# Sorted expert tiles: hidden units on the partitions, expert weights as the stationary operand

## The chip, the cores and the metric

The kernel runs on one core of a Trainium2 chip. The metric is the device time of one execution in microseconds; a time is the median of several runs. Engines run in parallel and meet at semaphores: TensorE (PE in the profile, its weight loads PEld), VectorE (DVE), ScalarE (ACT), GpSimd (POOL) and SyncE (SP), which issues DMAs. TensorE's granted clock stands in the profile as a share of 2.4 GHz: 1.00 is 2.4 GHz and 0.50 is 1.2 GHz, its two levels.

## The reference

Two graph layers, each followed by an expert network, run over 6250 rows of 256 numbers. The change lies in the last network, in which every row goes to the one expert of 32 that its router chooses:

```python
xf = x.reshape(-1, D)                              # layer-normed rows, D = 256
idx = jnp.argmax(xf @ router_w.T + router_b, axis=-1)
h = jnp.einsum('nd,ndh->nh', xf, W1[idx]) + b1[idx]   # 64 hidden units
h = jax.nn.relu(h)
out = jnp.einsum('nh,nhd->nd', h, W2[idx]) + b2[idx]
out = jax.nn.relu(out)                             # and x + out is the result
```

## The kernel before, in words

The kernel is written by hand, engine by engine: each block gives every engine its own list of instructions, and only semaphores order them between engines. Its stages follow one another: node features and edge scores, attention over the edges, the first expert network, the second sum over the edges (a gather stage, to about 2600 us in the profile), then `mean_route` and `expert_tiles`.

`mean_route` finishes the second graph layer, normalises it and routes the rows. In its first block SyncE loads the router's weights RWN, the vectors GA and BE and the router's bias RBB on one queue (L2136 to L2139). TensorE waits for both router loads before it transposes the router's weights (L2242). A middle part transposes and multiplies the rows for the router (L2356, L2368, L2380). At the end VectorE works out the place of every row in a list that is sorted by expert, padded to 128 rows for each expert, and for each of the TL = 80 tiles of that list the expert's number times 64 (TE1) and times 256 (TE2). GpSimd scatters the rows to that list in HBM (`rows_by_expert`, 49 indirect DMAs, L2303). The first-layer weights of all experts stand in SBUF as M1 (256 input features in two halves on the partitions, 32 x 64 columns), the second-layer weights and bias as M2 (64 + 1 partitions, 32 x 256 columns).

`expert_tiles` is the sorted-tile loop. SyncE first loads the first-layer bias of all experts, copied to all 128 partitions (B1B, L2538), and then keeps 16 tiles of 128 rows in flight (L2544). For each tile VectorE normalises (L2640), TensorE transposes both halves (L2566), ScalarE copies them to SBUF (xT, L2618), and TensorE multiplies with the tokens as stationary operand and the expert's 64 columns of M1 as moving operand, at an address from a register (L2578). So the product has tokens on its partitions. VectorE adds the bias (L2650), TensorE transposes the hidden rows (L2586), ScalarE applies the relu (L2626), and TensorE multiplies by the second layer (L2596), where a row of ones in hT brings in the bias b2. Ahead of that it computes another product of 256 columns into the other half of the same bank, which nothing reads (L2595). VectorE applies the relu and adds the row (L2657), and GpSimd scatters the result to its place in the output (L2551). Turn j of TensorE's loop works on four tiles: it transposes tile j, runs the first layer of tile j - 1, the hidden transpose of tile j - 2 and the second layer of tile j - 3. Every 16 tiles TensorE and VectorE load 16 registers each with the tiles' addresses (`load`). Buffers: two of xT, h, hT and of each PSUM tile, four of the outputs O and their row numbers ID.

All matrix products are in fp32; one such product stands in the trace as two records, a transpose as one.

Of the kernel before, what the change touches and what calls it, by code (L numbers as in the profile page):

```python
# [111 lines left out]
def program(nc, x, src, dst, edge_attr, W_fc, W_e, attn_h, attn_e, attn_t, bias, sW1, sb1, sW2, sb2, sW3, sb3,  # L112
# [16 lines left out]
    with ctx:  # L129
# [79 lines left out]
        POSI = sb(ctx, "POSI", [128, RB], i32)  # L209
        TE1 = sb(ctx, "TE1", [1, TL], i32)  # L210
# [3 lines left out]
        with phase():  # L214
            put = mean_route(nc, sb, ps, sem, sems, ACC, WM, IDF, RDQ, REAL, SKIPF, gamma, beta, W1, W2, b2, M1, M2, GX, ST, MEAN, RSTD,
                             ident, iota, below, epsc, router_w, router_b, POSI, TE1, TE2, SORTD)
            expert_tiles(nc, sb, ps, sem, sems, SORTD, put, TE1, TE2, M1, b1, M2, ident, out)

# [1872 lines left out]
def mean_route(nc, sb, ps, sem, sems, ACC, WM, IDF, RDQ, REAL, SKIPF, gamma, beta, W1, W2, b2, M1, M2, GX, ST, MEAN, RSTD, ident, iota,  # L2091
               below, epsc, router_w, router_b, POSI, TE1, TE2, SORTD):
# [11 lines left out]
    with ExitStack() as s:  # L2104
# [22 lines left out]
        with ExitStack() as one:  # L2127
# [5 lines left out]
            with nc.Block() as block:  # L2133
                @block.sync
                def _(sp):
                    sp.dma_start(RWN[:, :], router_w[:, :]).then_inc(rw_in, 16)  # L2136
                    sp.dma_start(GA[:, :], gamma.rearrange("(k p) -> p k", p=128), allow_slow_non_contiguous=True).then_inc(w_in, 16)
                    sp.dma_start(BE[:, :], beta.rearrange("(k p) -> p k", p=128), allow_slow_non_contiguous=True).then_inc(w_in, 16)
                    sp.dma_start(RBB[:, :], router_b.partition_broadcast(128)).then_inc(rw_in, 16)  # L2139
                    sp.wait_ge(w_in, 32)  # L2140
                    sp.wait_ge(rw_in, 32)

                @block.vector
                def _(dve):
# [38 lines left out]
                    dve.wait_ge(w_in, 32)  # L2183
# [93 lines left out]
        with nc.Block() as block:  # L2277
# [120 lines left out]
            def _(dve):  # L2398
# [101 lines left out]
                nc.vector.tensor_scalar(TEG[:, :], TEF[:, :], float(NE - 1), float(EH), ALU.min, ALU.mult)  # L2500
                dve.drain()
# [7 lines left out]

def expert_tiles(nc, sb, ps, sem, sems, SORTD, put, TE1, TE2, M1, b1, M2, ident, out):  # L2510

    S = 4
    TS = 16
    RG = 16
    with ExitStack() as s:
        B1B = sb(s, "B1B", [128, NE * EH])
# [11 lines left out]
        b_in, one_set = sem("b1_in"), sem("hT_ones")  # L2528
# [3 lines left out]
        h_psum, h_ready, r_psum, r_ready = sem("sh_psum"), sem("sh_ready"), sem("shT_psum"), sem("shT_ready")  # L2532
        o_psum, o_ready = sem("so_psum"), sem("so_ready")

        with nc.Block() as block:
            @block.sync
            def _(sp):
                sp.dma_start(B1B[:, :], b1.rearrange("e h -> (e h)").partition_broadcast(128)).then_inc(b_in, 16)  # L2538

                sp.wait_ge(put, 16 * RB)  # L2540
                for j in range(TL):
                    if j >= TS:
                        sp.wait_ge(o_ready, j - TS + 1)
                    sp.dma_start(T[j % TS][:, :], SORTD[j * 128:(j + 1) * 128, :]).then_inc(t_in[j % TS], 16)  # L2544
                sp.wait_ge(b_in, 16)
# [11 lines left out]
            def _(pe):  # L2557
                regs1 = [pe.alloc_register(f"te1_{m}") for m in range(RG)]
# [23 lines left out]
                def turn_hidden(j):  # L2582
                    pe.wait_ge(h_ready, j + 1)
                    if j >= 2:
                        pe.wait_ge(r_ready, j - 1)
                    nc.tensor.transpose(pR[j % 2][0:EH, 0:128], h[j % 2][:, :], ident[:, :]).then_inc(r_psum, 1)  # L2586

                def second_layer(j):
# [3 lines left out]
                    pe.wait_ge(r_ready, j + 1)  # L2592
                    if j >= 2:
                        pe.wait_ge(o_ready, j - 1)
                    nc.tensor.matmul(pO[j % 2][:, D:2 * D], xT[j % 2][:, 0:128], M1[:, 0, 0:D], start=True, stop=True)  # L2595
                    nc.tensor.matmul(pO[j % 2][:, 0:D], hT[j % 2][:, :],  # L2596
                                     M2[:, :, :].rearrange("h e d -> h (e d)")[:, ds(r, D)],
                                     start=True, stop=True).then_inc(o_psum, 1)

                pe.wait_ge(one_set, 2)  # L2600
                for j in range(TL + 3):
# [4 lines left out]
                    if 0 <= j - 2 < TL:  # L2606
                        turn_hidden(j - 2)
                    if 0 <= j - 3 < TL:
                        second_layer(j - 3)

            @block.scalar
            def _(act):
                for j in range(TL + 2):
                    if j < TL:
                        act.wait_ge(t_ready, j + 1)
                        if j >= 2:
                            act.wait_ge(h_psum, j - 1)
                        nc.scalar.activation(xT[j % 2][:, :], pT[j % 2][:, 0:KD * 128], ACT.Copy).then_inc(x_ready, 1)  # L2618
                    n = j - 2
                    if 0 <= n < TL:  # L2620
                        act.wait_ge(r_psum, n + 1)
                        if n >= 2:
                            act.wait_ge(o_psum, n - 1)
                        else:
                            act.wait_ge(one_set, 2)
                        nc.scalar.activation(hT[n % 2][0:EH, :], pR[n % 2][0:EH, 0:128], ACT.Relu).then_inc(r_ready, 1)  # L2626

            @block.vector
            def _(dve):
                for k in range(2):  # L2630
                    nc.vector.memset(hT[k][EH:EH + 1, :], 1.0).then_inc(one_set, 1)
                regs = [dve.alloc_register(f"tb1_{m}") for m in range(RG)]
                dve.wait_ge(b_in, 16)
# [9 lines left out]
                def hidden(j):  # L2643
                    if j % RG == 0:
                        dve.load(regs, TE1[0:1, j:j + RG])
                    r = dve.snap(regs[j % RG], min_val=0, max_val=(NE - 1) * EH)
                    dve.wait_ge(h_psum, j + 1)
                    if j >= 2:
                        dve.wait_ge(r_psum, j - 1)
                    nc.vector.tensor_tensor(h[j % 2][:, :], pH[j % 2][:, 0:EH], B1B[:, ds(r, EH)], ALU.add).then_inc(h_ready, 1)  # L2650

                def finish(j):
# [4 lines left out]
                    nc.vector.scalar_tensor_tensor(O[j % S][:, :], pO[j % 2][:, 0:D], 0.0, T[j % TS][:, 0:D],  # L2657
# [35 lines left out]
```

## Time and profile before

| | |
|---|---|
| median of 3 runs | 3021.5 us (3019.42 to 3024.75) |
| the profiled execution | 3018.93 us, span 3017.1 us |
| busy over the span | PE 2261.7 us (75%), PEld 1908.8 (63%), POOL 1837.4 (61%), DVE 1745.5 (58%), ACT 1283.2 (43%) |
| sorted-tile loop | from about 2857 us to the end of the span |

The shares are means over stages that have different limits, so what bears on the change is the stretch of the sorted-tile loop. Times in views count from the start of the span. A group's row gives the busy time of all its instructions, the mean of one in ns, and the idle time of its engine just before them with what ended it. A matmul's record includes the time until its result is out, so consecutive ones overlap; the chain of waits counts only what each adds. The columns of a window are: its stretch, its length, the busy us of PE, PEld, DVE, ACT and POOL with the number of their records, the granted clock, the mean busy share of the 16 DMA engines, and GB/s.

### The profile page before, as it was taken

What the parts mean: (1) busy time and instruction counts of PE and PEld (TensorE: products, weight loads), DVE (VectorE), ACT (ScalarE), POOL (GpSimd) and SP (SyncE); (2) the same over time, 40 slices, a digit from 0 to 9 for tenths busy, and PEclk for the clock granted to TensorE, in tenths of its full rate; (3) what the DMA queues carried; (4) which work ended last, traced back from release to release, by engine and by line L of the source; (5) the groups of instructions that cost most, each with busy time, mean ns of one, the idle gap of its engine ahead of it and who ended that gap; (6) DMA issues with size and microseconds to landing.
All of it is one profiled execution on the core that took longest, in us unless ns stands there. A gap on an engine that the chain in (4) does not pass through costs nothing. (4 is left out here: it accounts for less than half of the span.)

```text
span 3017.1 us, 46958 instructions
## 1 busy us (share of the span) xinstructions
PE 2261.7 (75%) x12072; PEld 1908.8 (63%) x12072; DVE 1745.5 (58%) x5695; ACT 1283.2 (43%) x4568; POOL 1837.4 (61%) x1935
## 2 busy tenths in 40 slices
PE   5987667666766666699994887788878887874098
PEld 4886566666665555588873665666666666763087
DVE  6433888888888888677763333333333333567054
ACT  1533555555555454455563333333333333442033
POOL 5575777777777777421216777777777777300655
PEclk8999788888888788899995657655665666787599
DMA  7698444444444445520002333333333333103342
GB/s 211 176 224 232 111 112 112 112 111 112 113 112 112 112 111 131 169 65 15 29 15 91 105 106 106 105 106 106 105 106 106 105 106 106 49 1 57 127 122 80
DMA packets 250114, 323.65 MB, mean 107 GB/s; under 512 B 152723, under 2 KB 181001, under 8 KB 249335
## 3 DMA queue, kind: packets, MB, share of 16 engines
q0 software_dynamic: 89424, 235.59, 27.7%
q1 hardware_dynamic: 155784, 82.05, 11.4%
q10 hardware_dynamic: 4640, 3.02, 0.5%
q8 instruction: 100, 1.64, 0.2%
q14 instruction: 166, 1.36, 0.1%
HBM read 276.41 MB, written 48.24 MB: 108 GB/s over the span
## 5 line engine op out<-in xcount | busy, mean ns | idle before, releaser
L1526 PE MATMUL pAb<-HOTb,Gb 128*128 128x128 f32 x3136 | 811.5, 412 | 203.9 <-DMA Gb<-normed_rows,SRCT 154.0
L1505 POOL DMA_INDIRECT Gb<-normed_rows,SRCT x784 | 741.3, 946 | 248.9 <-issue 238.5
L1526 PEld LDWEIGHTS pAb<-HOTb,Gb 128*128 128x128 f32 x3136 | 633.5, 286 | 382.3 <-DMA Gb<-normed_rows,SRCT 297.5
L1566 DVE TENSOR_TENSOR ACC<-ACC,pAb 128x256 f32 x784 | 330.5, 422 | 642.2 <-PE pAb L1526 569.1
L1093 POOL DMA_INDIRECT GX<-ft_rows,SRCT x432 | 413.1, 956 | 131.5 <-issue 129.0
L1179 ACT ACTIVATE ACC<-apA 128x254 f32 x784 | 300.4, 383 | 409.4 <-PE apA L1252 335.0
L1252 PE MATMUL apA<-AHOT,GX 128*128 128x129 f32 x1920 | 302.0, 326 | 83.5 <-DVE GX L1401 83.1
L1545 ACT ACTIVATE HOTb<-OFFb 128x1024 f32<-128x1024 f32 x98 | 103.6, 1057 | 604.4 <-PE pAb L1526 604.2
L1252 PEld LDWEIGHTS apA<-AHOT,GX 128*128 128x128 f32 x1920 | 286.7, 238 | 102.6 <-DVE GX L1401 102.6
L1093 POOL DMA_INDIRECT G<-ft_rows,SRCT x288 | 274.5, 953 | 87.6 <-issue 84.8
L1541 ACT ACTIVATE OFFb<-iota,NRELb 128x128 f32<-128x128 f32 x784 | 239.6, 388 | 6.7
L1252 PE MATMUL apA<-AHOT,G 128*128 128x129 f32 x1216 | 196.0, 332 | 50.6 <-DVE G L1401 48.6
L1252 PEld LDWEIGHTS apA<-AHOT,G 128*128 128x128 f32 x1216 | 186.0, 243 | 62.6 <-DVE G L1401 60.1
L1694 POOL DMA_INDIRECT normed_rows<-nrow,IDI x49 | 50.1, 1022 | 252.6 <-ACT nrow L1923 239.1
L1401 DVE TENSOR_TENSOR GX<-GX,apV 128x1024 f32<-128x1024 f32 x120 | 143.1, 1192 | 0.0
L1180 ACT ACTIVATE FL<-apA 128x4 f32<-128x4 f32 x784 | 135.1, 172 | 0.0
L2303 POOL DMA_INDIRECT rows_by_expert<-GX,POSI x49 | 48.6, 993 | 135.4 <-DVE POSI L2490 120.7
L2551 POOL DMA_INDIRECT out_dram<-sO,sID x80 | 77.7, 972 | 77.7 <-issue 40.9
L1301 DVE TENSOR_TENSOR AHOT<-apL,RELT 128x1024 f32<-128x1024 f32 x98 | 118.6, 1210 | 0.0
L2618 ACT ACTIVATE sxT<-spT 128x256 f32<-128x256 f32 x80 | 30.7, 383 | 164.5 <-PE spT L2566 164.5
L520 PE MATMUL pS<-VB,eT 128*128 128x128 f32 x784 | 98.6, 280 | 0.5 <-ACT V L617 0.5
L1159 ACT ACTIVATE ACC<-VAL 128x2 f32 x792 | 89.8, 196 | 11.9 <-ACT FL L1180 10.8
(416 smaller groups left out, 3981.6 us busy)
## 6 DMA issues: line engine op xcount, KB each, us to landing
ebuf<-in_edge_attr_dram SPq DMA_DIRECT2D x49, 448.0 KB
Gb<-normed_rows,SRCT POOLq DMA_INDIRECT x784, 2.7
rows_by_expert<-ffn_PADT SPq DMA_DIRECT2D x1, 10360.0 KB, 45.0
sT<-rows_by_expert SPq DMA_DIRECT2D x80, 129.5 KB, 2.1
GX<-ft_rows,SRCT POOLq DMA_INDIRECT x480
ft_rows<-row SPq DMA_DIRECT2D x25, 231.0 KB
GX<-in_x_dram SPq DMA_DIRECT2D x10, 560.0 KB
G<-ft_rows,SRCT POOLq DMA_INDIRECT x304
```

The costliest lines, as they stand in the source:

```text
L520: last = nc.tensor.matmul(pS[:, m * 2 * H0:m * 2 * H0 + 128], eT[c % 2][:, m * EP:(m + 1) * EP], VB[:, :], start=True, stop=True)
L1093: pool.indirect_dma_start(G[c % GS][:, m, :], None, FT[:, :], bass.IndirectOffsetOnAxis(ap=SRCT[:, t:t + 1], axis=0)).then_inc(g_in[c % GS ...
L1179: nc.scalar.activation(acc[:, :, ds(r + 1, EP - 1)], sums[:, :, 1:EP], ACT.Copy)
L1180: nc.scalar.activation(FL[:, :, f:n + 1:n - f], sums[:, :, 0:HW:EP], ACT.Copy).then_inc(pfree[b], 1)
L1252: last = nc.tensor.matmul(pA[b][:, f * HW:(f + 1) * HW], G[c % GS][:, m, f * 128:(f + 1) * 128], HOT[c % 2][:, m, :], start=True, stop=True)
L1301: nc.vector.tensor_tensor(HOT[c % 2][:, h * HT:(h + 1) * HT, 0:EP], pL[0:EP, 256:256 + EP].unsqueeze(1).to_broadcast([EP, HT, EP]), RELT[: ...
L1401: nc.vector.tensor_tensor(v, v, pV[0:EP, 0:128].rearrange("p (h m) -> p h m", m=UT)[:, :, m:m + WB].rearrange("p h m -> p m h").unsqueeze( ...
L1505: pool.indirect_dma_start(G[g % R][m][:, :], None, TABLE[:, :], bass.IndirectOffsetOnAxis(ap=SRCT[:, t:t + 1], axis=0)).then_inc(g_in[g % ...
L1526: last = nc.tensor.matmul(pA[b][:, o:o + EP], G[k][m][:, c * 128:(c + 1) * 128], HOT[k % 2][:, m, :], start=True, stop=True)
L1541: nc.scalar.activation(OFF[k2][:, m, :], iota[0:EP, 0:EP], ACT.Abs, bias=NREL[k2][:, m:m + 1])
L1545: nc.scalar.activation(HOT[k2][:, :, :], OFF[k2][:, :, :], ACT.Relu, bias=1.0, scale=-1.0).then_inc(hot[k2], 1)
L1566: last = nc.vector.tensor_tensor(acc[:, :, ds(b, EP)], acc[:, :, ds(b, EP)], pA[q][:, o:o + KD * EP].rearrange("p (c r) -> p c r", c=KD), ...
```

## The change

The first layer's product is turned round: for each tile ScalarE copies the expert's first-layer weights (128 partitions x 2 x 64 numbers) from M1 to a buffer WU, and the two 128x64 halves of WU become the stationary operand, with the 128 transposed tokens as moving operand. The product has the hidden units on its partitions, so the transpose of the hidden rows goes (with it L2586, pR and h), and so does VectorE's bias addition: ScalarE's relu reads the product from PSUM and takes the expert's bias as a column of B1T, a transposed copy of b1 with 64 partitions and 32 columns, addressed by the expert's plain number (TE0). SyncE loads B1T in the first block of `mean_route`, behind RWN and ahead of GA, BE and RBB; the broadcast load of B1B goes. The product that nothing reads goes. The loop has three stages in place of four; xT, hT, WU, pH and pO have three buffers, O, ID and xn six. The register load for the first layer moves from TensorE to ScalarE, and the one for the bias from VectorE to ScalarE.

The diff, cut to its core (the remaining lines pass B1T and TE0 through and rename semaphores):

```diff
 # program
+        B1T = sb(ctx, "B1T", [EH, NE])
+        TE0 = sb(ctx, "TE0", [1, TL], i32)
 # mean_route, first block, SyncE
                     sp.dma_start(RWN[:, :], router_w[:, :]).then_inc(rw_in, 16)
+                    sp.dma_start(B1T[:, :], b1.rearrange("e h -> h e"), allow_slow_non_contiguous=True).then_inc(w_in, 16)
 ...
-                    sp.wait_ge(w_in, 32)
+                    sp.wait_ge(w_in, 48)
 # mean_route, first block, VectorE
-                    dve.wait_ge(w_in, 32)
+                    dve.wait_ge(w_in, 48)
 # mean_route, end, VectorE
                 nc.vector.tensor_scalar(TEG[:, :], TEF[:, :], float(NE - 1), float(EH), ALU.min, ALU.mult)
+                nc.vector.tensor_scalar(TE0[:, :], TEF[:, :], float(NE - 1), None, ALU.min)
 # expert_tiles
-    S = 4
+    S = 6
+    W = 3
-        B1B = sb(s, "B1B", [128, NE * EH])
-        xT = [sb(s, f"sxT{k}", [128, KD * 128]) for k in range(2)]
-        h = [sb(s, f"sh{k}", [128, EH]) for k in range(2)]
-        hT = [sb(s, f"shT{k}", [EH + 1, 128]) for k in range(2)]
+        xT = [sb(s, f"sxT{k}", [128, KD * 128]) for k in range(W)]
+        WU = [sb(s, f"sWU{k}", [128, KD, EH]) for k in range(W)]
+        hT = [sb(s, f"shT{k}", [EH + 1, 128]) for k in range(W)]
-        pH = [ps(s, f"spH{k}", [128, 512]) for k in range(2)]
-        pR = [ps(s, f"spR{k}", [128, 512]) for k in range(2)]
-        pO = [ps(s, f"spO{k}", [128, 512]) for k in range(2)]
+        pH = [ps(s, f"spH{k}", [128, 512]) for k in range(W)]
+        pO = [ps(s, f"spO{k}", [128, 512]) for k in range(W)]
 # SyncE
-                sp.dma_start(B1B[:, :], b1.rearrange("e h -> (e h)").partition_broadcast(128)).then_inc(b_in, 16)
 # TensorE
                 def first_layer(j):
-                    if j % RG == 0:
-                        pe.load(regs1, TE1[0:1, j:j + RG])
-                    r = pe.snap(regs1[j % RG], min_val=0, max_val=(NE - 1) * EH)
                     pe.wait_ge(x_ready, j + 1)
-                    if j >= 2:
-                        pe.wait_ge(h_ready, j - 1)
+                    if j >= W:
+                        pe.wait_ge(h_ready, j - W + 1)
                     for c in range(KD):
-                        last = nc.tensor.matmul(pH[j % 2][:, 0:EH], xT[j % 2][:, c * 128:(c + 1) * 128], M1[:, c, ds(r, EH)],
-                                                start=(c == 0), stop=(c == KD - 1))
+                        last = nc.tensor.matmul(pH[j % W][0:EH, 0:128], WU[j % W][:, c, :],
+                                                xT[j % W][:, c * 128:(c + 1) * 128], start=(c == 0), stop=(c == KD - 1))
                     last.then_inc(h_psum, 1)
-                def turn_hidden(j):
 ...
-                    nc.tensor.transpose(pR[j % 2][0:EH, 0:128], h[j % 2][:, :], ident[:, :]).then_inc(r_psum, 1)
                 def second_layer(j):
 ...
-                    nc.tensor.matmul(pO[j % 2][:, D:2 * D], xT[j % 2][:, 0:128], M1[:, 0, 0:D], start=True, stop=True)
+                    nc.tensor.matmul(pO[j % W][:, 0:D], hT[j % W][:, :], M2[:, :, :].rearrange("h e d -> h (e d)")[:, ds(r, D)],
                                      start=True, stop=True).then_inc(o_psum, 1)
-                for j in range(TL + 3):
+                for j in range(TL + 2):
                     if j < TL:
                         turn(j)
                     if 0 <= j - 1 < TL:
                         first_layer(j - 1)
                     if 0 <= j - 2 < TL:
-                        turn_hidden(j - 2)
-                    if 0 <= j - 3 < TL:
-                        second_layer(j - 3)
+                        second_layer(j - 2)
 # ScalarE
-                for j in range(TL + 2):
+                regs = [act.alloc_register(f"tb1_{m}") for m in range(RG)]
+                regs1 = [act.alloc_register(f"te1_{m}") for m in range(RG)]
+                for j in range(TL + 1):
                     if j < TL:
+                        if j >= W:
+                            act.wait_ge(h_psum, j - W + 1)
+                        if j % RG == 0:
+                            act.load(regs1, TE1[0:1, j:j + RG])
+                        r = act.snap(regs1[j % RG], min_val=0, max_val=(NE - 1) * EH)
+                        nc.scalar.activation(WU[j % W][:, :, :], M1[:, :, ds(r, EH)], ACT.Copy)
                         act.wait_ge(t_ready, j + 1)
-                        if j >= 2:
-                            act.wait_ge(h_psum, j - 1)
-                        nc.scalar.activation(xT[j % 2][:, :], pT[j % 2][:, 0:KD * 128], ACT.Copy).then_inc(x_ready, 1)
-                    n = j - 2
+                        nc.scalar.activation(xT[j % W][:, :], pT[j % 2][:, 0:KD * 128], ACT.Copy).then_inc(x_ready, 1)
+                    n = j - 1
                     if 0 <= n < TL:
-                        act.wait_ge(r_psum, n + 1)
+                        if n % RG == 0:
+                            act.load(regs, TE0[0:1, n:n + RG])
+                        e = act.snap(regs[n % RG], min_val=0, max_val=NE - 1)
+                        act.wait_ge(h_psum, n + 1)
 ...
-                        nc.scalar.activation(hT[n % 2][0:EH, :], pR[n % 2][0:EH, 0:128], ACT.Relu).then_inc(r_ready, 1)
+                        nc.scalar.activation(hT[n % W][0:EH, :], pH[n % W][0:EH, 0:128], ACT.Relu,
+                                             bias=B1T[:, ds(e, 1)]).then_inc(h_ready, 1)
 # VectorE
-                def hidden(j):
 ...
-                    nc.vector.tensor_tensor(h[j % 2][:, :], pH[j % 2][:, 0:EH], B1B[:, ds(r, EH)], ALU.add).then_inc(h_ready, 1)
                 norm(0)
-                for j in range(TL + 3):
+                for j in range(TL + 2):
                     if j + 1 < TL:
                         norm(j + 1)
-                    if 0 <= j - 1 < TL:
-                        hidden(j - 1)
-                    if 0 <= j - 3 < TL:
-                        finish(j - 3)
+                    if 0 <= j - 2 < TL:
+                        finish(j - 2)
```

## Rows read from the trace of the kernel before

**Rows 1.** Chain of waits, one tile: start us, length us, engine, line.
```profile
2901.20 0.22 PE spT L2566 x2
2901.42 0.39 PE spH L2578 x4
2901.81 0.11 PE spR L2586
2901.92 0.43 PE spO L2595 x2
2902.35 0.43 PE spO L2596 x2
```

**Rows 2.** Chain of waits, longest pieces of the span; columns alike.
```profile
2857.07 4.79 DMA sT<-rows_by_expert
...
2869.44 0.85 PE spO L2596 x2
...
2895.65 0.65 PE spH L2578 x4
...
2922.65 0.65 PE spH L2578 x4
```

**Rows 3.** Windows: stretch, length, busy us by engine, clock, DMA share, GB/s.
```profile
2877.00:2878.00 1.00, 1.00 (x7) 0.97 (x7) 0.48 (x3) 0.50 (x2) 0.26 (x1) 0.70 0.03 6
2895.00:2915.00 20.00, 18.85 (x129) 16.93 (x130) 11.58 (x48) 7.67 (x24) 10.89 (x12) 1.00 0.42 120
```

**Rows 4.** Groups, 2865 to 3005: busy us, mean ns, idle before, releaser.
```profile
L2657 DVE SCALAR_TENSOR_TENSOR sO<-spO,sT 128x256 f32<-128x256 f32 x80 | 33.9, 424 | 53.3 <-PE spO L2596 53.3
...
L2640 DVE TENSOR_SCALAR sxn<-sT 128x256 f32<-128x256 f32 x77 | 31.1, 404 | 0.0
...
L2655 DVE CAST sID<-sT 128x1 int32<-128x1 f32 x80 | 11.5, 143 | 0.1
...
L2618 ACT ACTIVATE sxT<-spT 128x256 f32<-128x256 f32 x78 | 29.9, 383 | 70.7 <-PE spT L2566 70.7
...
L2626 ACT ACTIVATE shT<-spR 64x128 f32<-64x128 f32 x80 | 21.6, 270 | 17.2 <-PE spR L2586 8.9
```

**Rows 5.** Timeline of the loop: start us, length us, instruction, idle before.
```profile
2871.58 0.97 POOL L2551 DMA_INDIRECT out_dram<-sO,sID  x1 [19.22 <-DVE sO L2657]
...
2995.29 0.42 DVE L2657 SCALAR_TENSOR_TENSOR sO<-spO,sT 128x256 f32<-128x256 f32 x1 [0.59 <-PE spO L2596]
...
2996.50 0.97 POOL L2551 DMA_INDIRECT out_dram<-sO,sID  x1 [0.62 <-issue]
...
3006.79 0.97 POOL L2551 DMA_INDIRECT out_dram<-sO,sID  x1 [0.31 <-issue]
```

**Rows 6.** Groups by shape, ScalarE, whole span; columns as rows 4.
```profile
L1939 ACT ACTIVATE e<-fpM,ffn_C 128x256 f32<-128x256 f32 x144 | 67.2, 474 | 55.3 <-PE fpM L2034 31.1 <-PE fpM L2041 24.1
...
L1133 ACT ACTIVATE U_ex<-U_own 128x128 f32<-128x128 f32 x49 | 15.3, 312 | 0.0
```

**Rows 7.** DMA issues of the page: count, KB each, us to landing.
```profile
sT<-rows_by_expert SPq DMA_DIRECT2D x80, 129.5 KB, 2.1
```

**Rows 8.** Window at the opening of the mean stage.
```profile
2603.00:2608.00 5.00, 4.56 (x11) 3.69 (x12) 1.80 (x6) 2.57 (x5) 0.00 (x0) 0.51 0.12 15
```

**Rows 9.** Timeline of the same opening.
```profile
2605.00 0.47 SPq L2139 DMA_DIRECT2D RBB<-in_L_ffn_router_b_dram  x1
...
2610.80 0.31 PE L2242 MATMUL rpL<-ident,RWN 32*128 32x32 f32 x2
```

**Rows 10.** Windows in the gather stage and the router stage.
```profile
2475.00:2480.00 5.00, 2.80 (x16) 2.04 (x16) 2.11 (x5) 0.61 (x1) 3.78 (x5) 1.00 0.37 105
2480.00:2485.00 5.00, 3.99 (x17) 3.06 (x17) 1.27 (x3) 2.99 (x10) 3.78 (x5) 0.66 0.36 105
...
2682.00:2692.00 10.00, 7.25 (x58) 6.28 (x57) 7.04 (x25) 6.13 (x13) 0.00 (x0) 1.00 0.00 0
2692.00:2697.00 5.00, 1.21 (x11) 0.96 (x10) 4.31 (x11) 0.36 (x1) 0.00 (x0) 0.97 0.02 3
```

More of the change, by code:

```diff
@@ L215, in program @@
             put = mean_route(nc, sb, ps, sem, sems, ACC, WM, IDF, RDQ, REAL, SKIPF, gamma, beta, W1, W2, b2, M1, M2, GX, ST, MEAN, RSTD,
-                             ident, iota, below, epsc, router_w, router_b, POSI, TE1, TE2, SORTD)
-            expert_tiles(nc, sb, ps, sem, sems, SORTD, put, TE1, TE2, M1, b1, M2, ident, out)
+                             ident, iota, below, epsc, router_w, router_b, POSI, b1, B1T, TE0, TE1, TE2, SORTD)
+            expert_tiles(nc, sb, ps, sem, sems, SORTD, put, TE0, TE1, TE2, M1, B1T, M2, ident, out)
 def constants(nc, sem, ident, iota, below, epsc, FIRSTI):
@@ L2091, in mean_route @@
 def mean_route(nc, sb, ps, sem, sems, ACC, WM, IDF, RDQ, REAL, SKIPF, gamma, beta, W1, W2, b2, M1, M2, GX, ST, MEAN, RSTD, ident, iota,
-               below, epsc, router_w, router_b, POSI, TE1, TE2, SORTD):
+               below, epsc, router_w, router_b, POSI, b1, B1T, TE0, TE1, TE2, SORTD):
     K = 5
@@ L2507, in mean_route, with expert_tiles @@
     return put
-def expert_tiles(nc, sb, ps, sem, sems, SORTD, put, TE1, TE2, M1, b1, M2, ident, out):
-    S = 4
+def expert_tiles(nc, sb, ps, sem, sems, SORTD, put, TE0, TE1, TE2, M1, B1T, M2, ident, out):
+    S = 6
+    W = 3
     TS = 16
@@ L2531, in expert_tiles @@
         xn_ready, t_ready, x_ready = sem("sxn_ready"), sem("sxT_psum"), sem("sxT_ready")
-        h_psum, h_ready, r_psum, r_ready = sem("sh_psum"), sem("sh_ready"), sem("shT_psum"), sem("shT_ready")
+        h_psum, h_ready = sem("shT_psum"), sem("shT_ready")
         o_psum, o_ready = sem("so_psum"), sem("so_ready")
@@ L2544, in _ @@
                     sp.dma_start(T[j % TS][:, :], SORTD[j * 128:(j + 1) * 128, :]).then_inc(t_in[j % TS], 16)
-                sp.wait_ge(b_in, 16)
             @block.gpsimd
@@ L2557, in _ @@
             def _(pe):
-                regs1 = [pe.alloc_register(f"te1_{m}") for m in range(RG)]
                 regs2 = [pe.alloc_register(f"te2_{m}") for m in range(RG)]
@@ L2591, in second_layer @@
                     r = pe.snap(regs2[j % RG], min_val=0, max_val=(NE - 1) * D)
-                    pe.wait_ge(r_ready, j + 1)
-                    if j >= 2:
-                        pe.wait_ge(o_ready, j - 1)
-                    nc.tensor.matmul(pO[j % 2][:, D:2 * D], xT[j % 2][:, 0:128], M1[:, 0, 0:D], start=True, stop=True)
-                    nc.tensor.matmul(pO[j % 2][:, 0:D], hT[j % 2][:, :],
-                                     M2[:, :, :].rearrange("h e d -> h (e d)")[:, ds(r, D)],
+                    pe.wait_ge(h_ready, j + 1)
+                    if j >= W:
+                        pe.wait_ge(o_ready, j - W + 1)
+                    nc.tensor.matmul(pO[j % W][:, 0:D], hT[j % W][:, :], M2[:, :, :].rearrange("h e d -> h (e d)")[:, ds(r, D)],
                                      start=True, stop=True).then_inc(o_psum, 1)
-                pe.wait_ge(one_set, 2)
-                for j in range(TL + 3):
+                pe.wait_ge(one_set, W)
+                for j in range(TL + 2):
                     if j < TL:
@@ L2614, in _ @@
                     if j < TL:
+                        if j >= W:
+                            act.wait_ge(h_psum, j - W + 1)
[3 more added lines that the diff above has]
+                        nc.scalar.activation(WU[j % W][:, :, :], M1[:, :, ds(r, EH)], ACT.Copy)
                         act.wait_ge(t_ready, j + 1)
-                        if j >= 2:
-                            act.wait_ge(h_psum, j - 1)
@@ L2628, in _ @@
             @block.vector
             def _(dve):
-                for k in range(2):
+                for k in range(W):
                     nc.vector.memset(hT[k][EH:EH + 1, :], 1.0).then_inc(one_set, 1)
-                regs = [dve.alloc_register(f"tb1_{m}") for m in range(RG)]
-                dve.wait_ge(b_in, 16)
                 def norm(j):
@@ L2641, in norm @@
                                             ALU.subtract, ALU.mult).then_inc(xn_ready, 1)
-                def hidden(j):
[L2644 to L2649, printed above, removed]
-                    nc.vector.tensor_tensor(h[j % 2][:, :], pH[j % 2][:, 0:EH], B1B[:, ds(r, EH)], ALU.add).then_inc(h_ready, 1)
                 def finish(j):
```

12 lines of the change are left out of this document (5 added, 7 removed).

## The prediction

> **What bounds the kernel now.** I read the chain of waits first, since it says which engine the end hangs on. In the sorted-tile loop it is nearly all TensorE: one tile at the full clock is two transposes (0.22 us), the first layer (0.39), the transpose of the hidden rows (0.11), the product that nothing reads (L2595, 0.43) and the second layer (L2596, 0.43), 1.58 us together [rows 1]. The longest pieces add two things. The first sorted tile lands 4.79 us after its issue, and the pieces of a tile come twice as long early in the loop (0.85 against 0.43 for L2596). And from one 16-tile mark to the next the loop takes 2922.65 - 2895.65 = 27.00 us, which is 16 x 1.58 = 25.28 and 1.72 more: the two loads of 16 registers that TensorE makes there, some 0.86 us each [rows 2]. The windows say the same: from 2895 to 2915 TensorE is busy 18.85 of 20 us at granted clock 1.00 (2.4 GHz), VectorE 11.58, GpSimd 10.89, ScalarE 7.67; the rise from 1.2 GHz stands in the window from 2877 (mean 0.70) [rows 3]. So the loop is bound by TensorE's own work.
>
> Who is next? VectorE spends 0.424 + 0.404 + 0.143 = 0.97 us a tile on finish, norm and the index cast, ScalarE 0.383 + 0.270 = 0.65 [rows 4]. GpSimd's scatter of the result costs 0.97 us of issuing, and 0.31 of idle time when nothing holds it, 1.28 a tile, as at the last tile. When it has to wait, it starts 0.79 us after VectorE's finish (2995.29 + 0.42 to 2996.50). The first scatter starts at 2871.58, the last at 3006.79: 79 intervals of 1.711 us [rows 5].
>
> **The change, part by part.**
> TensorE loses the hidden transpose (0.11) and the unread product (0.43). The first layer keeps its four records, but each now has 64 stationary columns and streams 128 tokens instead of 64 columns: by L2596 (two records of 256 columns in 0.43) a 128-column record takes 0.107, four take 0.43, against 0.39 before, where the 128-column weight loads held it up [rows 1]. A tile comes to 0.22 + 0.43 + 0.43 = 1.08 us. One register load stays: 0.86 / 16 = 0.05. TensorE: 1.13 at the full clock, 2.21 at half.
>
> ScalarE gains a 128x128 copy from SBUF to SBUF; the nearest row takes 0.312 (an Exp of that shape). I take 0.31; the ends are 0.27 and 0.38, its 64x128 and 128x256 evictions. The relu gets a bias pointer: a 128x256 relu with bias took 0.474 where the copy without took 0.383, so 0.09 more, 0.36 [rows 4, 6]. Sum 0.31 + 0.38 + 0.36 = 1.05; two register loads per 16 tiles move to it, 2 x 0.86 / 16 = 0.11, so 1.16. Its new wait at the head of a turn is for a first layer three tiles back, long done; behind it queue the copies on which TensorE's next first layer depends.
>
> VectorE loses the bias addition and stays at 0.97. Its finish still waits for a free output slot, now one of six: six scatters are 7.7 us of GpSimd's time, so that wait can only pass on GpSimd's pace.
>
> So the four engines stand at 1.13, 1.16, 0.97 and 1.28. GpSimd becomes the bound, which no edit touches: 79 x 1.28 = 101.1 us from the first scatter to the last. TensorE's savings beyond 1.28 are lost; three buffers in place of two and six slots let the others run ahead and cover the register loads.
>
> The start: the 1 MB bias broadcast (128 partitions of 2048 words) that SP issued ahead of the sorted tiles goes. A tile's load has a median landing of 2.1 us, the first took 4.79 [rows 2, 7]; so the first lands at 2857.07 + 2.1 = 2859.2, 2.7 us sooner. If the broadcast was not what held it, nothing is gained; its own place on the queue may give another 0.4. From landing (2861.86) to the first scatter (2871.58) were 9.7 us, with four stages at half clock; now there are three, and a half-clock stage was 2 x 1.58 = 3.16 us of TensorE. With some 0.5 us for ScalarE's copy and loads I take 7.1: first scatter at 2866.3.
>
> The clock rose at about 2877.3, 15 us after TensorE's start; the same delay from 2859.8 gives 2874.6. Between 2866.3 and 2874.6 tiles come at 2.21 in place of 1.28: 3.8 tiles, 3.5 us more. If it rises at once, 0; if it takes twice as long, some 10.
>
> Before the loop: SP issues the transposed bias load (2048 words of four bytes) ahead of gamma, beta and the router bias, and TensorE waits for the router bias before it turns the router's weights at 2610.80. That bias was issued at 2605.00; landing by the median of rows 7 it was there at about 2607.6, so there are 3.2 us of cover. The window with the four loads of that place (by the code 672 short pieces) shows the DMA engines busy a share of 0.12 of its 5 us, 0.6 us; three times as many pieces are 1.8, plus one issue like the router bias's, 0.5: 2.3, covered. On only a quarter of the engines it would be 7.2 + 0.5, and 4.5 us would come through, since TensorE is busy 4.56 of 5 us there [rows 7 to 9]. I take nothing. VectorE's own wait on that semaphore stands behind the statistics of all blocks. The extra 80-element operation for the expert numbers stands behind the router's last step, while GpSimd still has most of its 49 scatters to issue: nothing, or some 0.15 us (the cast of rows 4) if that cover went.
>
> Sum: the last scatter starts at 2866.3 + 3.5 + 101.1 = 2970.9 instead of 3006.79, 35.9 us sooner; the tail behind it is unchanged. The profiled execution took 3018.93 us (span 3017.1), so it becomes 2983.0. It lies 2.6 us under the median of the runs, 3021.5; against that median I forecast 3021.5 - 35.9 = 2985.6.
>
> **Rivals.**
> *ScalarE's turn binds.* Its three steps follow one another, two behind TensorE; if each of these two hand-overs stays open by 0.15 us (about half of GpSimd's 0.31 of issue, the only issue gap shown in this loop), a tile takes 1.16 + 0.30 = 1.46, above GpSimd's 1.28 [rows 4 to 6]. Then 79 x 1.46 = 115.3, with 2.9 for the half clock 2984.5, 22.3 us gained: 2999. For it: waits and address arithmetic stand between all three. Against: all of the 70.7 us that ScalarE idles before its larger eviction now end with TensorE's transposes, none with an issue of its own.
>
> *The clock stays at half: the slower side.* The unread product is also dense work. Without it TensorE is paced by another engine, and there the clock may not hold: in the gather stage, paced by GpSimd, it was 1.00 from 2475 to 2480 with TensorE busy 2.80 of 5 us, then a mean of 0.66 in the next 5 [rows 10]. At 1.2 GHz all the way a tile takes 2.21: 79 x 2.21 = 174.6, the last scatter at 3040.9, 34 us later than now: 3056. It decides from the share s of the loop at half clock where 1.28 + 0.93 s exceeds the (3006.79 - 2866.3) / 79 = 1.778 us that would make no difference: s = 0.54. Against: at half clock TensorE is again the slowest engine and works without gaps, as it did when the clock rose at 2877; and in the router stage, of transposes and short products, it held 1.00 from 2682 to 2692 with TensorE busy 7.25 of 10 us, falling only behind a stretch of 1.21 in 5 [rows 3, 10]. The new loop leaves gaps of 1.28 - 1.08 = 0.2 us a tile. The Trainium skill speaks for this rival: TensorE: Matmul & The Clock Gate, Part 4, says that transposes do not count as busy for the clock the way products do. By that rule 0.22 of the 1.08 us would be lost to the clock, and if it went to half my sum would be the 3056 of this rival. The router stage, which by its code makes eight transposes beside every four products, held its clock all the same, so I give the rule little.
>
> *The transposed load is slow*, as priced above: 4.5 us of the gain go, 2990.
>
> **How the numbers follow.** Forecast 0.61; ScalarE's turn 0.25; half clock 0.09, of which 0.06 for well over half of the loop and 0.03 for about half; slow load 0.05. The range: below, the clock rises at once (3.5), the queue place (0.4) and the spread of the runs (about 3) lead to 2978; above it takes in ScalarE's turn with its pessimistic side, 1.50 a tile, 3003. The half clock stays outside. This kernel's measurement tells apart about 0.2%, 6 us: faster 0.91 (the forecast, ScalarE's turn and the slow load), same 0.03, slower 0.06 (the two parts of the half clock).
>
> **What would show it.** Right: scatters 1.28 us apart with 0.3 of idle time "issue" before each; in the chain GpSimd in place of TensorE; clock 1.00 from about 2875, TensorE idle some 0.2 us a tile; first scatter near 2866; the stages before the loop unchanged. Wrong: scatters 1.4 or more apart, with VectorE's finish as their releaser and ScalarE busy nearly throughout; a clock of 0.50 in the loop's windows; a wait of the router's transposes for a DMA near 2611.

## The result and the profile after

The changed kernel takes 3086.8 us (3079.6 to 3089.0), the kernel before 3022.1 beside it: a ratio of 1.021 [1.020, 1.023]. It is 65 us slower, where I forecast 36 us faster. The profiled execution took 3079.62 us, span 3077.8. The four executions are alike: their mean clock over the span is 0.735 to 0.747, where executions below whose clock rises in the loop have 0.761 or more.

Windows of the loop after the change (columns as in rows 3):

```profile
2870.00:2890.00 20.00, 20.00 (x62) 12.74 (x62) 6.07 (x23) 7.18 (x23) 7.61 (x8) 0.50 0.30 94
...
3040.00:3060.00 20.00, 20.00 (x62) 12.75 (x61) 5.65 (x21) 7.19 (x23) 7.77 (x8) 0.50 0.01 1
```

Against [rows 3] the clock is 0.50 (1.2 GHz) from the loop's first tiles to its last, though TensorE has a record in flight all the time; GpSimd is busy 7.6 to 7.8 of 20 us. The chain view of this trace ends at the last DMA, so the timeline stands in for it: the loop's first load and norm, the first scatter, TensorE and its weight loads over one tile, and the last scatter.

```profile
2852.38 3.67 SPq L2545 DMA_DIRECT2D sT<-rows_by_expert  x8
2854.59 0.41 DVE L2635 TENSOR_SCALAR sxn<-sT 128x256 f32<-128x256 f32 x1 [1.68 <-DMA sT<-rows_by_expert]
...
2861.99 0.97 POOL L2551 DMA_INDIRECT out_dram<-sO,sID  x1 [13.92 <-DVE sO L2643]
...
2949.69 0.63 PE L2565 MATMUL spT<-ident,sxn 128*128 128x128 f32 x2
2950.25 1.12 PE L2575 MATMUL spH<-sxT,sWU 128*64 128x128 f32 x4
2951.29 1.22 PE L2586 MATMUL spO<-ACC,shT 65*128 x2
2952.31 0.42 PE L2565 MATMUL spT<-ident,sxn 128*128 128x128 f32 x1
...
2950.25 0.71 PEld L2575 LDWEIGHTS spH<-sxT,sWU 128*64 128x64 f32 x4 [0.33 <-issue]
2951.29 0.50 PEld L2586 LDWEIGHTS spO<-ACC,shT 65*128 65x128 f32 x2 [0.33 <-issue]
...
3067.43 0.97 POOL L2551 DMA_INDIRECT out_dram<-sO,sID  x1 [0.30 <-issue]
```

From spT to spT a tile is 2952.31 - 2949.69 = 2.62 us. The streams alone, at the prediction's durations doubled for 1.2 GHz, are 2 x 1.08 = 2.16. The other 0.46 stands in the two PEld rows: the first weight load of the first layer, and the first of the second layer, begin only when their own matmul does, after 0.33 us with no load. The gaps stand where the operands change from 128 columns to 64 and back: the second of the two 64-column products loads right behind the first. In the kernel before the loads of both layers start ahead of their matmuls (2901.15 against 2901.26 and 2901.97 against 2902.19 in the tile of [rows 1]), without such a gap. From the first scatter (2861.99) to the last (3067.43) 79 intervals take 2.60 us each, against 1.711 in [rows 5].

The groups of the loop (columns as in rows 4, which they answer):

```profile
L2551 POOL DMA_INDIRECT out_dram<-sO,sID x78 | 75.8, 972 | 141.1 <-DVE sO L2643 141.1
L2575 PEld LDWEIGHTS spH<-sxT,sWU 128*64 128x64 f32 x312 | 55.8, 218 | 26.1 <-issue 26.1
L2586 PEld LDWEIGHTS spO<-ACC,shT 65*128 65x128 f32 x158 | 39.8, 313 | 26.0 <-issue 26.0
...
L2643 DVE SCALAR_TENSOR_TENSOR sO<-spO,sT 128x256 f32<-128x256 f32 x80 | 34.0, 425 | 145.9 <-PE spO L2586 145.9
...
L2611 ACT ACTIVATE sxT<-spT 128x256 f32<-128x256 f32 x77 | 29.5, 384 | 66.3 <-PE spT L2565 66.3
L2622 ACT ACTIVATE shT<-spH,B1T 64x128 f32<-64x128 f32 x79 | 28.6, 362 | 61.8 <-PE spH L2575 61.8
L2609 ACT ACTIVATE sWU<-ACC 128x128 f32 x77 | 22.9, 297 | 3.2 <-issue 3.2
```

All waits lead to TensorE: GpSimd waits for VectorE's finish, VectorE and ScalarE for matmuls. ScalarE's three steps cost 0.30, 0.38 and 0.36 us.

The balance of the last scatter, 3067.43 against 3006.79 in [rows 5], +60.6: the loop's first load is issued 4.7 us sooner (2852.38 against 2857.07 in [rows 2]; 0.4 is the place of the broadcast on the queue, the rest comes from the stages ahead of `mean_route`, which the change leaves alone), the first scatter comes another 4.9 sooner, and the 79 intervals take 205.4 us instead of 135.2, 70.2 more.

### The profile page after: what moved, and what is told of

It reads as the page before. It is cut to its first block and busy times, and to the rows that moved or that the text cites. A ratio compares the mean times of both kernels' runs of the same rounds, so it can differ in the third digit from the quotient of the medians.

```text
span 3077.8 us, 46081 instructions
## 1 busy us (share of the span) xinstructions
PE 2359.1 (77%) x11832; PEld 1939.7 (63%) x11832; DVE 1729.6 (56%) x5617; ACT 1307.4 (42%) x4648; POOL 1837.1 (60%) x1935
## 5 line engine op out<-in xcount | busy, mean ns | idle before, releaser
L1528 PE MATMUL pAb<-HOTb,Gb 128*128 128x128 f32 x3136 | 835.3, 422 | 179.9 <-DMA Gb<-normed_rows,SRCT 128.2
L1528 PEld LDWEIGHTS pAb<-HOTb,Gb 128*128 128x128 f32 x3136 | 651.5, 293 | 364.1 <-DMA Gb<-normed_rows,SRCT 280.2
L2643 DVE SCALAR_TENSOR_TENSOR sO<-spO,sT 128x256 f32<-128x256 f32 x80 | 34.0, 425 | 145.9 <-PE spO L2586 145.9
L2565 PE MATMUL spT<-ident,sxn 128*128 128x128 f32 x160 | 50.8, 420 | 80.6 <-DVE sxn L2635 80.6
L2565 PEld LDWEIGHTS spT<-ident,sxn 128*128 128x128 f32 x160 | 36.1, 228 | 103.5 <-issue 96.0
```

The costliest lines, as they stand in the source:

```text
L1528: last = nc.tensor.matmul(pA[b][:, o:o + EP], G[k][m][:, c * 128:(c + 1) * 128], HOT[k % 2][:, m, :], start=True, stop=True)
L2565: last = nc.tensor.transpose(pT[j % 2][:, c * 128:(c + 1) * 128], xn[j % S][:, c * 128:(c + 1) * 128], ident[:, :])
```

## The experiments

The theory after this reading: two things that the change took along, the unread product and the full width of the stationary operands, are what made TensorE fast, by the clock and by the weight loads. The rivals: the loop's other parts or the buffers keep the clock down; or the clock only has to be raised once.

**Put the unread product back**

```diff
 # after, second_layer
+                    nc.tensor.matmul(pO[j % W][:, D:2 * D], M1[:, 1, 0:128], M1[:, 0, 0:D], start=True, stop=True)
```

> The changed kernel with one unread product of 256 columns put back ahead of the second layer (constant operands). Theory A (the unread product is what brought the clock up and kept it): the clock rises to 1.00 within some 15 us of the loop's start and stays; a tile costs 1.08 + 0.43 = 1.51 us and perhaps 0.1 to 0.2 of uncovered weight loads, so 1.5 to 1.7; the whole 2990 to 3015 us. Theory B (the clock stays down because of the new first layer with its 64 stationary columns and weight loads that are no longer covered): 0.50 throughout, a tile 2.62 + 0.85 = 3.5 us, the whole about 3150 us.

Measured: 3033.5 us, ratio to before 1.0055 [1.0026, 1.0084]. Two windows around the rise, then one tile of TensorE and its loads:

```profile
2876.00:2878.00 2.00, 2.00 (x8) 1.35 (x7) 0.81 (x3) 0.38 (x1) 0.00 (x0) 0.50 0.22 74
...
2879.00:2880.00 1.00, 1.00 (x8) 0.71 (x7) 0.28 (x1) 0.32 (x3) 0.33 (x1) 1.00 0.25 87
...
2919.56 0.70 PE L2586 MATMUL spO<-ACC 128*128 128x256 f32 x2
...
2921.43 0.70 PE L2586 MATMUL spO<-ACC 128*128 128x256 f32 x2
...
2920.84 0.41 PEld L2575 LDWEIGHTS spH<-sxT,sWU 128*64 128x64 f32 x4 [0.17 <-issue]
2921.42 0.30 PEld L2586 LDWEIGHTS spO<-ACC 128*128 128x128 f32 x2 [0.17 <-issue]
```

The clock reaches 1.00, 18 us after TensorE's first work in the loop (2860.16 to 2878.6), and so it does in all six executions (mean clock 0.764 to 0.779). So theory A has the clock right. It has the time wrong: 3033.5 lies above its 2990 to 3015, since a tile is 1.87 us (2921.43 - 2919.56) where it had 1.5 to 1.7. That is 0.36 above the streams' 1.51 (1.08 + 0.43): the uncovered loads cost at the full clock too.

**Take the unread product out of the kernel before**

```diff
 # before, second_layer
-                    nc.tensor.matmul(pO[j % 2][:, D:2 * D], xT[j % 2][:, 0:128], M1[:, 0, 0:D], start=True, stop=True)
```

> The kernel before without its unread product, nothing else changed. Theory A: the clock stays at 0.50, a tile costs 3.09 - 0.85 = 2.24 us or somewhat more, the whole 3055 to 3085 us. Theory B: the clock rises as before, a tile costs 1.58 - 0.43 = 1.15 of TensorE's time, so GpSimd's 1.28 or somewhat more, and the whole is 2985 to 3000 us.

Measured: 3060.2 us, 1.013 [1.011, 1.015]. A late window and one tile's loads:

```profile
2950.00:2970.00 20.00, 20.00 (x82) 17.42 (x82) 9.11 (x37) 5.89 (x18) 8.77 (x9) 0.50 0.35 104
...
2950.43 0.28 PEld L2586 LDWEIGHTS spR<-ident,sh 128*64 128x64 f32 x1
2950.64 0.55 PEld L2595 LDWEIGHTS spO<-ACC,shT 65*128 65x128 f32 x2
```

Without the product the old loop stays at 0.50 as well, as theory A said. A product that nothing reads was worth 38 us to the kernel before. Its layers' loads follow one another without a gap, that of the 64-column transpose of the hidden rows too; so uncovered loads of the layers are not needed for a clock that stays down.

**First-layer weights 128 columns wide**

```diff
 # after
-        WU = [sb(s, f"sWU{k}", [128, KD, EH]) for k in range(W)]
+        WU = [sb(s, f"sWU{k}", [128, KD, 128]) for k in range(W)]
 ...
 # ScalarE, once ahead of the loop
+                    nc.scalar.activation(WU[k][:, :, EH:128], M1[:, :, 0:128 - EH], ACT.Copy)
 # TensorE, first_layer
-    nc.tensor.matmul(pH[j % W][0:EH, 0:128], WU[j % W][:, c, :],
+    nc.tensor.matmul(pH[j % W][:, 0:128], WU[j % W][:, c, :],
```

> The changed kernel with the stationary operand of the first layer filled up to 128 columns (the upper 64 are constant numbers, their product is not read). Streamed columns stay the same. Theory A (what counts is the product left out): clock 0.50, a tile about 2.6 us, about 3086 us. Theory B (64 stationary columns or the weight loads that go with them): the clock rises, a tile 1.3 us, about 2985 us. In both the gap of 0.33 us in the weight loads ahead of the first layer shows whether it hangs on the width of 64.

Measured: 2986.7 us, 0.988 [0.986, 0.990]: within noise the fastest of all, and 1 us from the forecast for the change itself. A window, one tile of TensorE with its loads, and two scatters:

```profile
2880.00:2890.00 10.00, 9.67 (x70) 8.37 (x70) 7.13 (x26) 7.02 (x25) 7.82 (x8) 1.00 0.66 185
...
2920.40 0.38 PE L2565 MATMUL spT<-ident,sxn 128*128 128x128 f32 x2
...
2921.51 0.38 PE L2565 MATMUL spT<-ident,sxn 128*128 128x128 f32 x2
...
2920.52 0.52 PEld L2575 LDWEIGHTS spH<-sxT,sWU 128*128 128x128 f32 x4
...
2920.62 0.61 PE L2575 MATMUL spH<-sxT,sWU 128*128 128x128 f32 x4
...
2920.96 0.30 PEld L2586 LDWEIGHTS spO<-ACC,shT 65*128 65x128 f32 x2
2921.07 0.60 PE L2586 MATMUL spO<-ACC,shT 65*128 x2
...
2922.50 0.97 POOL L2551 DMA_INDIRECT out_dram<-sO,sID  x1 [0.30 <-DVE sO L2645]
2923.78 0.98 POOL L2551 DMA_INDIRECT out_dram<-sO,sID  x1 [0.30 <-issue]
```

The records of the first layer are as many and as long; only the stationary operand is wider. Both loads now start ahead of their matmuls, the tile is 1.11 us where 1.08 was worked out, the clock rises (at 2871.8, 4 us after TensorE's first work), and GpSimd's scatters come 1.28 us apart. So here theory B's numbers come out, where the two runs before spoke for A: the product put back brings the clock up with the narrow operand, and the wide operand brings it up without the product.

**Raise the clock ahead of the loop**

```diff
 # after: TensorE, in its idle stretch of the last scatters to the sorted list
+                pe.wait_ge(warm, 1)
+                for n in range(24):
+                    nc.tensor.matmul(bank[4][:, 0:D], ident[:, :], WM[:, n % KD, :], start=True, stop=True)
...
 # expert_tiles, TensorE, ahead of the first tile
+                for n in range(8):
+                    nc.tensor.matmul(pO[W - 1][:, D:2 * D], M1[:, 1, 0:128], M1[:, 0, 0:D], start=True, stop=True)
```

> The changed kernel with TensorE kept at work by 24 unread products of 256 columns during the last scatters of the sorted list, where it is idle, and 8 more at the head of the loop, so that the loop starts at 1.00. Theory C (the loop can't raise the clock but can keep it): 1.00 throughout, scatters 1.28 to 1.35 us apart, the whole 2970 to 2985 us. Theory A or B as they stand (this loop's work is too little to hold the clock): it falls back to 0.50 within a few us of the loop's start, the whole 3075 to 3090 us.

Measured: 3000.3 us, 0.993 [0.991, 0.995]. A late window, one tile's transposes and loads, and VectorE's norm from 2880 to 2980:

```profile
2950.00:2960.00 10.00, 10.00 (x57) 6.93 (x57) 6.54 (x22) 6.63 (x22) 6.81 (x8) 1.00 0.56 168
...
2920.12 0.38 PE L2571 MATMUL spT<-ident,sxn 128*128 128x128 f32 x2
...
2921.55 0.38 PE L2571 MATMUL spT<-ident,sxn 128*128 128x128 f32 x2
...
2920.43 0.41 PEld L2581 LDWEIGHTS spH<-sxT,sWU 128*64 128x64 f32 x4 [0.17 <-issue]
2921.01 0.30 PEld L2592 LDWEIGHTS spO<-ACC,shT 65*128 65x128 f32 x2 [0.17 <-issue]
...
L2643 DVE TENSOR_SCALAR sxn<-sT 128x256 f32<-128x256 f32 x68 | 35.7, 525 | 0.0
```

The loop's own work holds the clock once it is up: theory C has that right. It has the time wrong, 2985 us at most, since the scatters come 1.46 us apart ((2988.47 - 2873.11) / 79) and not 1.28 to 1.35. Of the added products only the eight at the head raised the clock that the loop found, at 2866.5; the 24 had raised it too, but TensorE then idled for 15.57 us, and from 2850 on it stood at 0.50 again. What the uncovered loads cost at the full clock can be read alone: 2921.55 - 2920.12 = 1.43 us a tile against 1.08, 0.35; TensorE, not GpSimd, sets the pace.

**The unread product in the first 12 tiles only**

```diff
 # after, second_layer
+                    if j < 12:
+                        nc.tensor.matmul(pO[j % W][:, D:2 * D], M1[:, 1, 0:128], M1[:, 0, 0:D], start=True, stop=True)
```

> The changed kernel with the unread product of 256 columns in the first 12 tiles only. Theory (raising the clock needs the extra product, holding it does not): the clock rises near 2879 us as with the product in every tile, then stays at 1.00 without it; 68 tiles at 1.46 in place of 1.865 us make 3033.5 - 68 x 0.405 = 3006 us. Rival (the extra product is needed throughout): the clock falls back to 0.50 near 2890 us, 68 tiles at 2.60, 3033.5 + 68 x 0.735 = 3083 us.

Measured: 3008.1 us, 0.996 [0.994, 0.998]; the theory said 3006. The clock is up early, and still up long after the last of the 12 products. The rise, the first unread product, and a late window:

```profile
2864.90:2866.00 1.10, 1.10 (x7) 0.91 (x6) 0.00 (x0) 0.56 (x2) 0.00 (x0) 1.00 0.85 259
...
2864.85 0.70 PE L2587 MATMUL spO<-ACC 128*128 128x256 f32 x2
...
2950.00:2960.00 10.00, 10.00 (x58) 6.94 (x57) 6.53 (x22) 6.35 (x20) 6.80 (x8) 1.00 0.56 169
```

The 3006 came out partly by luck, for the rise was not as the theory had it. The clock rises at 2864.8, 14 us sooner than with the product in every tile, and just as the first unread product starts (2864.85). Up to there TensorE's work is that of the changed kernel, so the product can hardly be what raised it here. A start like the changed kernel's can, it seems, raise the clock by itself, though in none of its four executions did it. And the rise isn't certain with the product either. One of the seven executions, which the ratio leaves out, took 3096.6 us at a mean clock of 0.740. It has no windows, but 12 products at half clock on top of the changed kernel's time, 3086.8 + 12 x 0.86 = 3097.1 us, is what a clock that never rose would give by estimate.

**Wide weights, with the gaps brought back**

```diff
 # wide weights, first_layer, ahead of its products
+                    nc.tensor.matmul(pH[j % W][0:EH, 128:160], M1[:, 1, 0:EH], M1[:, 0, 0:32], start=True, stop=True)
```

> The changed kernel with 128-column first-layer weights, and ahead of each first layer a product of 64 stationary and 32 moving columns that nothing reads. Its narrow stationary operand brings the two uncovered weight loads back, 0.17 us each at the full clock, 0.33 at half. Theory A (the clock rises because the products fill the array): it rises near 2875 us all the same, a tile takes 1.10 + 0.05 + 0.34 = 1.49 us, some 3004 us. Theory B (it rises because TensorE's stream has no gaps): it stays at 0.50, a tile takes 2.20 + 0.10 + 0.66 = 2.96 us, some 3110 us. If a narrow operand does not uncover the loads after all: as without the extra product, 2987 us.

Measured: 3103.0 us, 1.026 [1.023, 1.028]; theory B said 3110. A window, and one tile:

```profile
2910.00:2920.00 10.00, 10.00 (x38) 7.36 (x37) 3.23 (x12) 3.65 (x12) 2.91 (x3) 0.50 0.28 78
...
2945.64 1.06 PE L2587 MATMUL spO<-ACC,shT 65*128 x2
...
2948.43 1.06 PE L2587 MATMUL spO<-ACC,shT 65*128 x2
...
2947.05 0.29 PEld L2574 LDWEIGHTS spH<-ACC 128*64 128x64 f32 x2 [0.33 <-issue]
2947.41 0.93 PEld L2576 LDWEIGHTS spH<-sxT,sWU 128*128 128x128 f32 x4
```

All that the wide version has is still there, and 32 moving columns more; yet the clock never leaves 0.50. Two loads again start with their matmuls (2947.05 and 2947.41; the first with 0.33 of idle time), and the tile is 2.79 us (2948.43 - 2945.64), where the streams, 2.16 and 0.11 for the added product (64 columns, an eighth of the second layer's 0.86), make 2.27. The full array alone doesn't raise the clock. The added product is itself narrow and short, and no run parts that from the gaps that it brings.

**Zeros in the added columns**

```diff
 # wide weights, ScalarE, once ahead of the loop
-    nc.scalar.activation(WU[k][:, :, EH:128], M1[:, :, 0:128 - EH], ACT.Copy)
+    nc.scalar.activation(WU[k][:, :, EH:128], M1[:, :, 0:128 - EH], ACT.Copy, scale=0.0)
```

> The changed kernel with 128-column first-layer weights, the upper 64 columns filled with zeros in place of numbers. Theory A (what counts is how many columns the operand has): clock and time as with numbers there, 2987 us. Rival C (the numbers count, products with zeros do not raise the clock): the loads stay covered but the clock stays at 0.50, a tile takes 2.20 us, 79 x 2.20 = 174 us of scatters, some 3056 us.

Measured: 2987.7 us, 0.988 [0.986, 0.991], as with numbers. The window from 2880 to 2890:

```profile
2880.00:2890.00 10.00, 9.99 (x72) 8.24 (x70) 7.47 (x28) 7.58 (x25) 7.56 (x9) 1.00 0.70 203
```

The wide loop doesn't hold the clock all the time: in this trace TensorE is busy only 1.24 of 2 us from 2912 to 2914, and from 2914.7 to 2918.1 the clock is at 0.50, then at 1.00 again. It costs nothing that shows: the 79 intervals of the scatters take 102.1 us here and 102.0 with numbers.

**96 columns instead of 128**

```diff
-        WU = [sb(s, f"sWU{k}", [128, KD, 128]) for k in range(W)]
+        WU = [sb(s, f"sWU{k}", [128, KD, 96]) for k in range(W)]
 ...
```

> The changed kernel with first-layer weights 96 columns wide, the upper 32 filled once with constant numbers whose product nothing reads. Theory F (only an operand of the full 128 columns lets the weight loads run ahead): as with 64 columns, two uncovered loads a tile, clock 0.50, tile 2.60 us, 3087 us. Theory W (64 columns, half of the array, is the special case): as with 128 columns, clock 1.00 from about 2875 us, scatters 1.28 us apart, 2987 us.

Measured: 2987.2 us, 0.987 [0.985, 0.990]: theory W. The loads run ahead, the second layer's right behind the first layer's:

```profile
2930.50 0.49 PEld L2575 LDWEIGHTS spH<-sxT,sWU 128*96 128x96 f32 x4
2930.93 0.30 PEld L2586 LDWEIGHTS spO<-ACC,shT 65*128 65x128 f32 x2
```

**Unread transposes instead of the unread product**

```diff
 # after, second_layer
+                    for n in range(4):
+                        nc.tensor.transpose(pO[j % W][:, D + n % 2 * 128:D + (n % 2 + 1) * 128], M1[:, 1, n * 128:(n + 1) * 128], ident[:, :])
```

> The changed kernel with four transposes of constant numbers that nothing reads (128 columns each, 0.43 us together at the full clock) ahead of each second layer, where an earlier run had one unread product of 256 columns, 0.43 us as well, and its clock rose. Theory (a transpose counts for the clock as a product does): the clock rises near 2879 us, tile 1.43 + 0.43 = 1.86 us, 3033 us. Rival (only products count): it stays at 0.50, a tile takes 2.60 + 0.86 = 3.46 us, 79 x 0.86 = 68 us more than the changed kernel, some 3155 us.

Measured: 3031.0 us, 1.0015 [1.0004, 1.0026]. The windows before and after the rise, and the first unread transposes:

```profile
2868.00:2869.00 1.00, 1.00 (x5) 0.67 (x6) 0.00 (x0) 0.41 (x2) 0.00 (x0) 0.50 0.92 262
...
2868.90 0.78 PE L2587 MATMUL spO<-ident,ACC 128*128 128x128 f32 x4
...
2870.00:2872.00 2.00, 2.00 (x15) 1.47 (x13) 0.84 (x4) 0.94 (x3) 0.60 (x1) 1.00 0.73 220
```

The time is the theory's, and the clock is up in all ten executions (mean 0.763 to 0.776), against none of the changed kernel's four, which were not timed beside these. That count speaks for the transposes. The one rise in the trace does not: it comes at 2869.2, 0.3 us behind the start of the first four and 10 us sooner than the theory had it, much as in the run with the product in the first 12 tiles, where no unread work had run yet. The Trainium skill, TensorE: Matmul & The Clock Gate, Part 4, has it that transposes don't count as busy for the clock the way products do; by the ten executions these fp32 transposes do count, so that rule is unlikely to be why the changed loop stays down.

**Wide weights and the clock raised ahead**

The two edits above, the wide weights and the products ahead of the loop, together.

> The changed kernel with 128-column first-layer weights, and with 24 unread products in TensorE's idle stretch ahead of the loop and 8 at its head. Theory (GpSimd's 1.28 us a tile binds, the clock only delays the start): full clock from the first tile on saves the half-clock start, 2 to 5 us, so 2982 to 2985 us; scatters 1.28 us apart. Rival (the start is hidden by GpSimd or the extra products delay it): 2987 us or more.

Measured: 2988.4 us, 0.988 [0.986, 0.991], no better than wide weights alone: the rival. The first and the last scatter:

```profile
2873.74 0.97 POOL L2557 DMA_INDIRECT out_dram<-sO,sID  x1 [14.71 <-DVE sO L2653]
...
2975.12 0.97 POOL L2557 DMA_INDIRECT out_dram<-sO,sID  x1 [0.30 <-issue]
```

79 intervals in 101.38 us are 1.283 each. In the version without the raised clock they are 2873.52 to 2975.53, 1.291: GpSimd sets the pace from its first scatter on, and there is next to nothing left for TensorE to give.

## Why the prediction was wrong

*The step that failed first*: "the same delay from 2859.8 gives 2874.6". I carried the rise of the clock over from a loop with the unread product to one without it. The clock stood at 0.50 to the loop's end. The two runs that add or remove only that product show what it did: the changed kernel's clock rises with it in six executions of six, and that of the kernel before doesn't without it in four of four. The slower rival had the mechanism ("the unread product is also dense work") and its 3056; I gave it 0.09 because the loop would be gapless at half clock, and because the router stage held 1.00 with little work. The first argument failed twice. The kernel before without its unread product has no idle time ahead of its layers' loads and stays at 0.50; and the new loop does have gaps. The second took holding for raising: the new loop too holds the clock once it is up.

*The term that was mis-sized*: "a 128-column record takes 0.107, four take 0.43", with loads covered, so 1.08 us a tile. The streams were right, but the first of the two products with a 64-column stationary operand has its first weight load uncovered, and so has the 128-column product behind them: 1.43 at the full clock, 2.62 at half. This put the result 30 us beyond the rival's 3056: 79 x (2.60 - 2.21) = 31 us. Even at the full clock the change would have brought about 3000 (the run with the clock raised ahead, whose products hold back the first transposes by 2.6 us), not 2985.6.

Either of the two mended alone brings the clock back. Put the product back and leave the operand narrow, and it rises though the gaps are still there (3033.5). Widen the operand to 96 or 128 columns without the product, and the loads are covered, the clock rises by itself, and 65 us of loss become 35 of gain; a small narrow product with its gaps in the wide version loses both again. So in the new loop neither the gaps nor the missing product keeps the clock down alone: the run with the product has the gaps, the wide one lacks the product. The old loop without its product stays down with its layers' loads covered, so there is more than one way to a clock that stays down. What the chip counts stays open, and so does how often the changed kernel's own start would raise the clock: four executions are too few to say never.

The rest of the working, by its own steps:
- GpSimd as the next bound, 1.28 us a tile: shown by the wide version (scatters 1.28 apart with 0.30 of idle time), 79 x 1.291 = 102.0 us against 101.1.
- ScalarE 0.31, 0.38 and 0.36: 0.30, 0.38 and 0.36. Its turn didn't bind where TensorE was fast: the rival at 1.46 is refuted by the wide version's pace.
- The first tile: landing in 2.1 us, measured 2.2 (2852.38 to 2854.59); 7.1 us from there to the first scatter, measured 7.4.
- The 3.5 us for tiles at half clock: gone in the wide version, since its clock is up before the first scatter and GpSimd's scatters come at their own pace from there, and the start with a raised clock gains nothing.
- The transposed bias load: costs next to nothing. The transposes of the router's weights wait 0.17 us for an issue and for no DMA, as this row of the changed kernel's trace has it, and from TensorE's first product of that stage they are 7.46 us away (2599.05 to 2606.51) against 7.36 before (2603.44 to 2610.80):

```profile
2606.51 0.20 PEld L2245 LDWEIGHTS rpL<-ident,RWN 32*128 32x128 f32 x2 [0.17 <-issue]
```

## What to carry to other kernels

Before taking work off TensorE, ask what it does for the clock: a product that nothing reads was worth 38 us here, and dropping it, right by every busy time, lost more than the saved columns brought. A narrow stationary operand isn't cheaper than a wide one if its load no longer runs ahead: look at the weight loads for idle time named "issue", and try padding it. A clock that rose in one trace may not rise in the next execution of the same kernel, so count executions before taking one rise for the work of an edit. "Busy 20.00 of 20" beside a clock of 0.50 is not a TensorE at its limit.

## What the runs showed of the hardware

- Where fp32 products go over from a 128-column stationary operand to 64 columns, and where they go back, the first weight load starts only with its matmul: in the changed loop 0.17 us without a load each time at 2.4 GHz, 0.33 at 1.2 GHz, 0.35 and 0.46 us of a tile for the two. Between two 64-column products there is no such gap. With 96 or 128 columns the loads run ahead; so did the load of a 64-column transpose in the kernel before. The Trainium skill, TensorE: Matmul & The Clock Gate, Part 2, says that the next tile's weights load while this tile's matmul runs, where the load's place in the array allows it; at these changes of width they don't, elsewhere in the layers they do.
- A loop can stay at 1.2 GHz for 205 us with a TensorE record always in flight, and the same loop keeps 2.4 GHz once it has it (100 us and more, until its end, in both traces that show it).
- With the same work from the loop's start on, the clock rose 4.8 us after TensorE's first transposes in one execution and 18 us after them in another (the product in the first 12 tiles, and in every tile).
- Zeros in the operand's added columns do for the clock what numbers do (2987.7 and 2986.7 us).
- VectorE's 128x256 norm took 525 ns on average in the loop that ran at 1.43 us a tile, against 404 in the kernels before and after. It isn't on the path there; what lengthens it wasn't tried.
